# Decoder layer on one core: the next pair's attention on VectorE split into three pieces, and sigmoid's activation table named after each Ln/Exp pair

## What is computed

```python
def _layernorm(x, axis=-1, eps=1e-05):
    ...
for _ in range(NUM_ITERS):                       # 3
    sn = rmsnorm(slots, slot_norm_w)
    q_proj = sn @ Wq.T
    scores = einsum('bkd,bmd->bkm', q_proj, k_proj) * SCALE
    attn = softmax(scores, axis=-2)              # over the 1024 slots
    attn = attn / (sum(attn, axis=-1, keepdims=True) + EPS)
    updates = einsum('bkm,bmd->bkd', attn, v_proj)
    slots = gru_cell(updates, slots, ...)        # r, z: sigmoid; n: tanh
x = _layernorm(x + slots)
# then: 8 experts, one chosen per token, and a last layer norm
```

## Time and profile before

| | |
|---|---|
| median of 3 runs | 638.34 us (637.24 to 638.39) |
| the profiled execution: its time | 638.83 us |
| its span, first to last instruction | 637.1 us |
| TensorE busy (matmul) | 546.8 us, 86% |
| VectorE / ScalarE / GpSimd busy | 457.4 / 373.3 / 253.5 us |
| granted TensorE clock, mean | 0.922 |

### The profile page before, as it was taken

One profiled execution on the slowest core, in us unless ns is written; L12 is line 12 of the kernel. 1 busy time (PEld: TensorE's weight loads), 2 busy tenths in 40 slices (PEclk: granted clock), 3 DMA queues, 4 the chain that ended last, 5 costly groups with the idle time before them and its releaser, 6 DMA issues.

```text
span 637.1 us, 7357 instructions
## 1 busy us (share of the span) xinstructions
PE 546.8 (86%) x2158; PEld 402.8 (63%) x2158; DVE 457.4 (72%) x806; ACT 373.3 (59%) x661; POOL 253.5 (40%) x239
## 2 busy tenths in 40 slices
PE   6999897597799979997997999799989886858781
PEld 3474536265578857876785788578878764636560
DVE  3999899985894995799489758964756579653431
ACT  4558195865665846584666668475756544634542
POOL 1032302021042564456454744543443462554453
PEclk9999897679899989998999999899999997878776
DMA  8921003010110000000000000020110724145421
GB/s 296 329 82 66 1 0 132 0 68 0 67 66 1 1 1 1 1 0 1 1 0 1 1 1 1 1 66 24 42 51 26 254 102 125 69 127 141 121 77 34
DMA packets 23896, 37.88 MB, mean 59 GB/s; under 512 B 3246, under 2 KB 15663, under 8 KB 23601
## 3 DMA queue, kind: packets, MB, share of 16 engines
q1 hardware_dynamic: 20448, 28.98, 14.5%
q0 software_dynamic: 3408, 8.43, 3.7%
HBM read 23.60 MB, written 14.72 MB: 60 GB/s over the span
## 4 chain that ended last, share of the span: by engine, by line
PE 46%; DVE 19%; issue 10%; ACT 8%; another core or an unknown queue 1%; POOL 0%; ACTq 0%; DVEq 0%; POOLq 0%
PE psum L1409 25%; PE psum L1481 7%; PE psum L1334 4%; DVE slots_full L1824 2%; DVE gru L1822 2%; DVE gru L1797 2%; PE psum L1454 2%; DVE at L1788 2%; PE psum L1158 2%; DVE sc L1779 2%; PE psum L1379 2%; DVE at L1790 2%; DVE ss_part L1755 1%; PE psum L1228 1%; PE psum L1247 1%
## 5 line engine op out<-in xcount | busy, mean ns | idle before, releaser
L1409 PE MATMUL psum<-slots_hi,w_hh 128*128 128x512 f32 x576 | 189.3, 411 | 15.3 <-DVE gru L1797 12.0
L1409 PEld LDWEIGHTS psum<-slots_hi,w_hh 128*128 128x128 f32 x576 | 109.4, 194 | 42.8 <-DVE gru L1797 13.7
L1015 POOL TENSOR_TENSOR gru<-slots_full,gru 128x512 f32<-128x512 f32 x43 | 67.8, 1576 | 161.7 <-ACT gru L744 161.6
L1409 PE MATMUL psum<-slots_lo,w_hh 128*128 128x512 f32 x288 | 116.7, 405 | 0.0
L1409 PE MATMUL psum<-at,v_ih_pair 128*128 128x512 f32 x288 | 92.9, 404 | 2.1 <-DVE at L1790 2.1
L1797 DVE SCALAR_TENSOR_TENSOR gru<-psum,vec,gru 128x512 f32<-128x512 f32 x48 | 35.9, 748 | 46.7 <-PE psum L1409 40.1
L1481 PE MATMUL psum<-slots_full,w_tile 128*128 x156 | 54.2, 482 | 14.7 <-issue 8.5
L1409 PEld LDWEIGHTS psum<-at,v_ih_pair 128*128 128x128 f32 x288 | 54.8, 193 | 17.1 <-DVE at L1790 3.9
L744 ACT ACTIVATE gru<-gru,vec 128x512 f32<-128x512 f32 x48 | 34.7, 723 | 52.3 <-DVE gru L1804 51.5
L1409 PEld LDWEIGHTS psum<-slots_lo,w_hh 128*128 128x128 f32 x288 | 55.8, 194 | 13.4
L1145 PE MATMUL psum<-early_hi,w_in 128*128 128x512 f32 x128 | 57.6, 608 | 5.1 <-DMA early_hi<-in_xT 4.9
(11 more groups left out here) (250 smaller groups left out, 1015.3 us busy)
## 6 DMA issues: line engine op xcount, KB each, us to landing
gathered<-sorted_rows SPq DMA_DIRECT2D x39, 129.0 KB, 1.9
x_scratch<-slots_full SPq DMA_DIRECT2D x8, 512.0 KB, 3.0
x_block<-x_scratch SPq DMA_DIRECT2D x8, 512.0 KB
early_hi<-in_xT SPq DMA_DIRECT2D x3, 1024.0 KB, 5.7
x_tm<-in_x SPq DMA_DIRECT2D x4, 512.0 KB, 6.9
slots_full<-in_expertT SPq DMA_DIRECT2D x1, 2048.0 KB, 11.1
sorted_rows<-gru SPq DMA_DIRECT2D x1, 1032.0 KB, 12.1
early_hi<-in_xT SPq DMA_DIRECT2D x2, 512.0 KB, 4.3
```

Source lines behind the costliest of these rows:

```text
L1015: pool.tensor_tensor(DF(u), full[:, c, seq(k, h), blk(j)], X(u), ALU.subtract).then_inc(d_pool, 1)
L1409: last = pe.matmul(psum[:, bank, :], w, d, start=start and i == 0, stop=stop and i == len(pairs) - 1)
```

## The change

`attention` keeps its multiplication and is moved ahead of `settle(k, 5)`; the rest of it becomes `spread_attention(f, h)`, for h = 0 right behind it, and for h = 1 after `settle(k, 6)`. `rms` and `normaliser` end with a request for sigmoid_and_others, a set that has tanh as well.

```diff
@@ -716,6 +716,7 @@ rms(f)
                     act.activation(inv[:], inv[:], ACT.Exp, scale=-0.5).then_inc(rstd_done, 1)
+                    act.preload_act_table_set("sigmoid_and_others")
@@ -1779,16 +1781,17 @@ attention(f)
                     dve.wait_ge(attn_done, f + 1)
-                    for h in range(2):
-                        n = 2 * f + h
-                        a = at[n % 3]
-                        mine, other = half(h), half(1 - h)
-                        if n > 2:
-                            dve.wait_ge(z_mm, U * (n - 2))
-                        dve.tensor_copy(a[mine, :], sc[mine, :]).then_inc(at_hi, 1)
-                        dve.wait_ge(at_hi, n + 1)
-                        dve.tensor_tensor(a[other, :], sc[mine, :], a[mine, :].bitcast(F32),
-                                          ALU.subtract).then_inc(at_lo, 1)
+
+                def spread_attention(f, h):
+                    n = 2 * f + h
+                    a = at[n % 3]
+                    mine, other = half(h), half(1 - h)
+                    if n > 2:
+                        dve.wait_ge(z_mm, U * (n - 2))
+                    dve.tensor_copy(a[mine, :], sc[mine, :]).then_inc(at_hi, 1)
+                    dve.wait_ge(at_hi, n + 1)
+                    dve.tensor_tensor(a[other, :], sc[mine, :], a[mine, :].bitcast(F32),
+                                      ALU.subtract).then_inc(at_lo, 1)
@@ -2057,10 +2062,12 @@ steps 1 to 4 (step 0 alike)
                     candidate(k, 6)
+                    attention(k + 1)
+                    spread_attention(k + 1, 0)
                     settle(k, 5)
-                    attention(k + 1)
                     candidate(k, 7)
                     settle(k, 6)
+                    spread_attention(k + 1, 1)
                     if later:
                         ss_low(k + 2, 2)
```

More of the change, by code:

```diff
@@ L2032, in _ @@
                 candidate(0, 6)
+                attention(1)
+                spread_attention(1, 0)
                 settle(0, 5)
-                attention(1)
                 candidate(0, 7)
                 settle(0, 6)
+                spread_attention(1, 1)
                 ss_low(2, 2)
```

## The result

**654.51 us** (median of 4 runs, 651.98 to 656.16) against 637.79 for the kernel before (4 runs, 636.31 to 638.39): ratio 1.026, 95% interval 1.022 to 1.030. The change makes the kernel slower by 16.7 us. The forecast was 652 with a range of 641 to 658. The profiled execution took 656.16 us with a span of 654.4; the one before 638.83 and 637.1.

What follows compares the result with a forecast made beforehand. The prediction took a VectorE chain from 338.7 to 363.2, with TensorE's wait inside it, as the bound. Chain 5.6, clock 3.2 and last step 4.6 summed to +13.4 on 638.3, giving 652 us, range 641 to 658.

Steps and rivals of the forecast that it cites:

- C: Rival: chain as forecast, clock never falls (648.5 us) or always falls, step 5 too (657); chance 0.25 for both ends.
- one to three falls: Main forecast: TensorE's clock falls behind the mean_squares wait in some of four steps, two taken, +3.2 us; chance 0.45.
- First part and HN: VectorE's attention up to HN of each step's first unit: stall 0.7 us instead of 3.4, 2.9 gained, no clock fall.
- The table requests: ScalarE: nine loads fewer, 11.5 us, count nothing in the sum because they lie beside the path, covered by the squares.
- Second part: VectorE from candidate(2, 7) to candidate(3, 0): 1.0 us idle for r_gate, GpSimd collisions, +0.4; TensorE waits 2.1 at unit (3,1).
- rival A: Faster, 625 us: GpSimd misses VectorE before candidate(3, 0), new waits do not form, 4.5 gained in each of four steps; chance 0.14.
- Third part: VectorE from candidate(3, 0) to ss_low m = 3: 10.9 or 11.0 us for 9.9; mean_squares +1.4 per step, four times, 5.6.
- The clock: TensorE's clock falls behind the 4.1 us wait before mean_squares, 1.6 each: bounds 0 and 6.4, two of four taken, +3.2.
- the chain hid the whole price of each fall: In the kernel before, the clock fall at HN preceded the VectorE chain's end, which hid its 1.6 us.
- Step 4: Last step: gate_centre ends at 471.0, not 466.3, +4.6 us, bounds 3.6 and 4.9; first token tile waits 6.5, not 1.85.
- the +2.1 of the sum: Step 4 of the recurrence: the attention's second rest, 1.2 us alone, is lengthened by 2.1 behind GpSimd's add_x1.
- 1.85 did not, 3.0 did: Clock reasoning: a TensorE wait of 3.0 us with 0.4 ahead lowered the clock; after one of 1.85 it stayed up.

Runs made afterwards that it cites:

- experiment 1: Kernel before plus only the two requests for sigmoid's table behind the Exps: ratio 1.0011 to the kernel before.
- experiment 2: Changed kernel without the two table requests, so VectorE's new order alone: ratio 1.0297 to the kernel before.
- Experiment 11: Changed kernel with GpSimd's low cut to 8 of its 512 columns: 622.93 us, ratio 1.0029 to the kernel before.
- experiment 3: Changed kernel with r_gate(k,7) ahead of squares(k,2) on ScalarE: ratio 1.0259 to the kernel before.
- Experiment 9: Changed kernel whose TensorE repeats matmuls in its two waits of each of steps 1 to 4: ratio 1.0165 to the kernel before.
- Experiment 4: Changed kernel with step 4 alone in the order of before: ratio 1.0172 to the kernel before.
- experiment 10: Kernel before with GpSimd's low cut to 8 of its 512 columns: 607.33 us, ratio 0.9782 to the kernel before.
- experiment 6: Changed kernel with mean_squares m=3 behind part XN of unit 2, not behind part R: ratio 1.0112 to the kernel before.
- Experiment 7: Kernel before with table requests and the attention's second half behind candidate(k,2) in steps 1 to 4: ratio 0.9947 to the kernel before.
- Experiment 12: Changed kernel, second half behind candidate(k,2), r_gate(k,7) before squares, mean_squares behind XN, old step 4, ss_low m=3 before unit 0's mix: 601.28 us, ratio 0.9681.
- experiment 8: Changed kernel, second half behind candidate(k,2), r_gate(k,7) ahead of squares(k,2), mean_squares m=3 behind XN, step 4 as before: ratio 0.9841 to the kernel before.

## Why the prediction was right, and where it was off

The sign and the mechanism held: +13.4 forecast, +17.3 between the two profiled executions and +16.7 between the medians. What came is the upper end of C, "always falls, step 5 too" (657), and not the forecast's one to three falls; that the time lies within 3 us of 652 is in part luck, since the chain cost less than forecast and the clock more. By terms:

- **First part and HN.** Forecast 0.7 us of stall for 3.4 and no fall of the clock there; it is 0.73 (1.29 in step 1), and the clock stays up. The gain at HN was real (2.7 us of TensorE's time in each step) and was all given back: two later waits on the same VectorE chain took it.
- **The table requests.** Costed at nothing with the squares as their cover. Experiments 1 and 2 show it from both sides: D moves by 0.1.
- **Second part.** Unit (k+1,1)'s HN waits 2.0 (forecast 2.1), VectorE idles 0.97 for r_gate (1.0), and the collisions came where they were forecast: unit 6's mix 1.16 and 1.67 us for 0.7 each, the second copy 1.68. Right in its sizes. But I gave its collisions the deciding role: rival A was to win if GpSimd missed VectorE there. Experiment 11 takes most of `low` away, and 3.7 of the chain's 5.0 us stay, with two waits of 1.0 on VectorE in place of collisions; experiment 3 takes one of these waits away, and a collision fills it. So waits and collisions stand in for each other, and neither alone decides. Both removed together was not tried on the new order as it stands.
- **Third part.** Forecast +1.4 per step. From `candidate(3, 0)` to the end of `ss_low` it took 10.8 us (forecast 10.9 or 11.0), without the pause and with unit (3,0)'s mix at 1.56 and 1.67. Experiment 9, where the clock does not fall, has a step of 60.46 against 58.98: +1.5. But four times 1.4 was one too many. At `mean_squares` of step 1 the new kernel is only 0.6 later (245.91 against 245.30, and 0.14 of that is its start), and in step 4 the kernel before reached it at 423.27 and not at 422.27, since the clock had stayed low for 6.8 us behind HN of unit (4,0), where it does so for 3.4 in the other steps, and VectorE waited 1.91 us for TensorE at unit (4,1) for 0.79. My reading that the chain hid the whole price of each fall holds for three of the four. In D the chain is 14.4 - 6.0 - 4.5 = 3.9, or 4.9 without that 1.0, not 5.6.
- **The clock: the term that was mis-sized.** I took two falls of four, 3.2. It fell behind `mean_squares` in all four steps, 6.0 by experiment 9, near the upper bound of 6.4. The wait there was forecast at 4.1; it is 3.74 where the clock had stayed up at unit 1 (step 4) and 2.2 where it had fallen (steps 1 to 3), since the first fall is absorbed in the second wait. One more fall stands behind the first token tile (480.91, four matmuls in 1.28 us, 0.74 before):

```profile
482.00:484.00 2.00, 2.00 (x6) 0.50 0.44 169
484.00:486.00 2.00, 2.00 (x8) 0.50 0.00 0
486.00:488.00 2.00, 2.00 (x12) 0.91 0.00 0
```

It lasts 6.8 us, twice as long as those in the steps. The stages behind the first tile are 2.8 us longer (654.4 - 480.91 against 637.1 - 466.38). Pairs of runs on one chip, with and without such a fall, differ there by 3.1 (experiments 2 and 1), 2.4 (2 and 4) and 3.2 (11 and 10), so this fall is about the whole of it, where C had 1.6. One run doesn't fit: experiment 6 has the same fall, and its stretch is only 1.0 us above that of the kernel before.
- **Step 4.** Forecast +4.6, with bounds 3.6 and 4.9. Experiment 4 gives 4.5. VectorE's copy and rest behind unit 6's mix, then GpSimd's `add_x1` (L1039):

```profile
475.73 1.64 DVE L1791 CAST at<-sc 64x1024 fp32r<-64x1024 f32 x1
477.40 3.25 DVE L1793 TENSOR_TENSOR at<-sc,at 64x1024 fp32r<-64x1024 f32 x1
```
and

```profile
476.78 2.79 POOL L1039 TENSOR_TENSOR slots_full<-slots_full,x_block 128x1024 f32<-128x1024 f32 x1
```

`add_x1` ends at 476.78 + 2.79 = 479.57, and the rest, asked for at 477.40, ends 1.08 later: it stood for all that `add_x1` had left. So the full wait behind `add_x1`, not the short one of the lower bound, is what happens: 3.25 us for 1.22, the +2.1 of the sum. The Trainium skill (SBUF — State Buffer, section SBUF: two separate sides) has the later one blocked for the whole of the earlier one; the trace agrees.

The sum in D: 3.9 + 6.0 + 4.5 = 14.4, and 2.8 behind it. Forecast: 5.6 + 3.2 + 4.6. The chain's error of 1.7 and the clock's of 2.8 stood against each other in part; the 2.8 behind the first tile had no term in the forecast.

## What to carry to other kernels

A wait that the busiest engine shows inside a longer chain of another engine is not a gain to be had: price the chain to its last link, and ask where the engine will wait when the first wait is gone. Here the cure was to move what is needed late (the attention's second half) out of the chain, into a stretch where VectorE waits for TensorE, to run ahead of a mix the one instruction that the chain ends on (`ss_low`), and to put TensorE's dependent matmuls behind work that it has anyway. Experiments 7, 12 and 6 price these three; r_gate ahead of the squares, which is in the fastest version too, brought nothing alone. When a waiting engine's clock can fall, each wait has a second price, paid only where the engine itself sets the time behind it; filling the wait with matmuls that are done over again measures it cleanly.

## What the runs showed that I had not expected

- **The same wait brings the clock down in one step and not in the next.** Behind the first token tile's wait of 1.85 or 1.86 it stayed up before and in experiments 1, 4 and 10, and fell in 7, 8 and 12 (0.59 in the 2 us behind it in 8). Of the changed kernel's four waits of 2.0 at unit 1 three were followed by a fall; of experiment 7's four of 2.6 one; of experiment 3's four of 2.7 three; of experiment 8's four of 1.90 two. The four of 3.0 before and all those of 3.7 were followed by one. My step "1.85 did not, 3.0 did" drew a line between two rows that the runs do not show.
- **A fall lasts 3.4 us or 6.8.** Worked out from the granted clock of 2 us windows, every low stretch from step 1 to the first token tile's, in all fourteen traces, has one of these two lengths.
- **GpSimd's `low` costs the kernel before 14 us**, 2.2%, though no entry in TensorE's list of waits names it: VectorE is 2.5 us less busy per step when it is cut (43.73 against 46.25).

```profile
290.76:349.74 58.98, 46.25 (x52) 0.97 0.00 1
```

- **One chip is 16 us slower on the same kernel** (636.9 against 620.9 and 621.7), all of it behind the first token tile: that stretch is 618.8 - 465.38 = 153.4 us in experiment 1 and 170.7 for the kernel before in the profile shown ahead, 156.5 in experiment 2 and 173.5 in the changed kernel. D is the same to 0.2 us. A lower granted clock goes with it: over the same 574 matmuls of the stretch it is 0.92 and 0.86, and TensorE is busy for 119.0 and 127.9 us; in the second pair 0.90 and 0.87, 122.0 and 126.6. That is 8.9 and 4.6 of the 17 us. What brings the clock down there, and the rest, is open.
